# Difference products in the second attention: scores of a key tile added to those of the tile two before, still in the bank

## The reference, cut to what matters

```
q = (text_hidden @ Wq) -> (b, 16, 256, 128)
k = (vision_tokens @ Wk), v = (vision_tokens @ Wv) -> (b, 8, 1601, 128), each used by two heads
scores = q k^T / sqrt(128);  attn = softmax(scores);  out = (attn v) @ Wo
```

## Time and profile before

| | us |
|---|---|
| median of 3 runs | 1743.28 |
| runs | 1741.46 to 1745.71 |
| the profiled execution | 1741.94 |
| its span (first to last instruction) | 1740.6 |

### The profile page before, as it was taken

One profiled execution on the slowest core, in us unless ns is written; L12 is line 12 of the kernel. 1 busy time (PEld: TensorE's weight loads), 2 busy tenths in 40 slices (PEclk: granted clock), 3 DMA queues, 4 the chain that ended last, 5 costly groups with the idle time before them and its releaser, 6 DMA issues.

```text
span 1740.6 us, 26277 instructions
## 1 busy us (share of the span) xinstructions
PE 1568.9 (90%) x8998; PEld 750.3 (43%) x8998; DVE 1290.8 (74%) x2579; ACT 1067.6 (61%) x1766; POOL 746.3 (43%) x571
## 2 busy tenths in 40 slices
PE   5788988989968799789999999999989999999989
PEld 3243343333323343224444554544544555455455
DVE  5777667767777146578889869899688886788937
ACT  3467767767756545447766656656567665666734
POOL 0013014014020012046687747776476665566723
PEclk8799999999989799979999999999999999999989
DMA  3000000000020130100000000000000000000000
GB/s 130 1 1 1 20 1 2 21 1 2 2 79 2 55 124 19 28 20 1 20 20 30 1 1 25 1 8 23 1 1 1 2 1 1 1 1 1 1 0 25
DMA packets 15883, 29.36 MB, mean 17 GB/s; under 512 B 2594, under 2 KB 12934, under 8 KB 14726
## 3 DMA queue, kind: packets, MB, share of 16 engines
q1 hardware_dynamic: 15750, 27.68, 4.7%
HBM read 26.53 MB, written 1.15 MB: 16 GB/s over the span
## 4 chain that ended last, share of the span: by engine, by line
PE 43%; DVE 7%; issue 5%; ACT 3%; POOL 1%; DMA 0%; DVEq 0%; POOLq 0%; ACTq 0%
PE BK L488 42%; DVE arena L1601 4%; DVE arena L1624 2%; ACT arena L1703 1%; POOL arena L1740 1%; ACT arena L1707 1%; DVE arena L1593 0%; ACT L1703 0%; ACT L731 0%; PE BK L1524 0%; PE BK L747 0%; DVE arena L1610 0%; ACT arena L1693 0%; DVE arena L1607 0%; DVEq L424 0%
## 5 line engine op out<-in xcount | busy, mean ns | idle before, releaser
L488 PE MATMUL BK<-arena 128*128 128x512 bf16 (+9 forms) x8670 | 1525.1, 370 | 115.0 <-DVE arena L1601 24.3
L488 PEld LDWEIGHTS BK<-arena 128*128 128x128 bf16 (+5 forms) x8670 | 715.3, 113 | 894.4 <-issue 263.1
L1740 POOL TENSOR_TENSOR arena<-arena 128x512 f32<-128x512 f32 (+1 forms) x352 | 505.4, 1436 | 224.0 <-ACT arena L1703 206.1
L1624 DVE TENSOR_TENSOR arena<-arena 128x512 bf16<-128x512 f32 (+1 forms) x416 | 431.0, 1040 | 23.4 <-ACT arena L1707 22.1
L1703 ACT ACTIVATE arena<-BK,arena 128x512 f32<-128x512 f32 (+1 forms) x416 | 285.8, 687 | 253.4 <-PE BK L488 253.4
L994 DVE TENSOR_REDUCE arena<-BK 128x1 f32<-128x512 f32 x384 | 251.2, 685 | 46.0 <-PE BK L488 44.2
L1136 ACT ACTIVATE arena<-BK 128x512 f32<-128x512 f32 (+1 forms) x416 | 225.7, 595 | 91.0 <-PE BK L488 86.2
L1601 DVE CUSTOM_DVE_ANT_0 arena<-BK,arena 128x512 bf16<-128x512 f32 x384 | 262.5, 684 | 22.8 <-PE BK L488 5.9
L1707 ACT CAST arena<-arena 128x512 bf16<-128x512 f32 (+1 forms) x416 | 257.1, 618 | 13.3
L1168 POOL TENSOR_TENSOR arena<-arena 128x256 f32<-128x256 f32 (+6 forms) x45 | 30.2, 672 | 180.6 <-ACT arena L1084 178.3
L1190 POOL TENSOR_TENSOR arena<-arena 128x512 bf16<-128x512 f32 x24 | 28.5, 1192 | 177.2 <-DVE arena L973 177.2
(11 more groups left out here) (150 smaller groups left out, 812.2 us busy)
## 6 DMA issues: line engine op xcount, KB each, us to landing
arena<-in_ctxT SPq DMA_DIRECT2D x8, 800.5 KB, 6.0
arena<-in_ctxk SPq DMA_DIRECT2D x4, 768.0 KB
arena<-in_wqT SPq DMA_DIRECT2D x1, 2048.0 KB, 10.2
arena<-in_wo SPq DMA_DIRECT2D x1, 2048.0 KB, 14.7
arena<-in_x SPq DMA_DIRECT2D x4, 256.0 KB, 11.3
arena<-in_rsel SPq DMA_DIRECT2D x1, 1024.0 KB, 9.5
arena<-in_rw1T SPq DMA_DIRECT2D x1, 1024.0 KB, 5.1
arena<-in_rwgT SPq DMA_DIRECT2D x1, 1024.0 KB, 7.6
```

The source lines that it names most:

```text
L488: return T.matmul(out_, lhsT, rhs, start=start, stop=stop, skip_group_check=True)
L1624: V.tensor_tensor(Pl[k][0:m, :], P1[k][0:m, :], Ph[k][0:m, :], ALU.subtract).then_inc(p_low, 1)
L1740: G.tensor_tensor(acc[0:m, g % 2, :], acc[0:m, g % 2, :], P1[k][0:m, :], ALU.add).then_inc(summed1, 1)
```

## The change

In the second attention, key tiles 0 and 1 are made as before, with the row of maxima as the first of their four products. From tile 2 on, three products are added (`start=False`) to the bank that still holds the scores of tile kt - 2, with the difference of the two context tiles in place of the context: differences `dch` (high part) and `ctl` (low part, columns from 256 on). The product with the row of maxima is made for kt 0 and 1 alone. The bank is now `kt % 2`, so kt 12 of one group and kt 0 of the next are both in bank 0.

The differences are made in the stage of the experts. `cx` now has on DVE: the cast to `cth`, a wait for POOL's low part of the first 256 columns, the difference of 1345 columns in float32 in place (in `ctf`), and its cast to `dch`; on POOL: the low part of the first 256 columns, and after DVE's cast that of the 1345. The context pieces start at step 12 (`s >= E - 4`), since three of the `dch` lie where the weights of the folding are, so `cx` falls behind `up` of steps 16, 21, 26 and 31.

Two more edits: `o1a` makes one column a product in place of 128, and the ternary intermediates `qa` and `qb_` become bfloat16.

```diff
@@ stage1
-            next(cside, None)
+            if s >= E - 4:
+                next(cside, None)
@@ stage2
-                piece("s1", s, bank=ntile[0] % 2)
-                ntile[0] += 1
+                piece("s1", s, bank=kt % 2)
@@ buffers
+        dch = [sb(f"dch{b}", [128, S2 - 256], BF16, L1) for b in range(3)] + [sb("dch3", [128, S2 - 256], BF16, MN)]
-        qa = sb("qa", [128, 1024], F32, L1)
-        qb_ = sb("qb_", [128, 1024], F32, L1)
+        qa = sb("qa", [128, 1024], BF16, L1)
+        qb_ = sb("qb_", [128, 1024], BF16, L1)
@@ vector_moe, piece cx
                     V.tensor_copy(cth[:, b, :], ctf[b % 2]).then_inc(ct_high, 1)
+                    dve.wait_ge(ct_done, 2 * b + 1)
+                    V.tensor_tensor(ctf[b % 2][:, 0:S2 - 256], ctf[b % 2][:, 256:S2], ctf[b % 2][:, 0:S2 - 256],
+                                    ALU.subtract).then_inc(ct_step, 1)
+                    dve.wait_ge(ct_step, b + 1)
+                    dve.wait_ge(*emptied("fold", H - 1))
+                    V.tensor_copy(dch[b][:, :], ctf[b % 2][:, 0:S2 - 256]).then_inc(ct_step_high, 1)
@@ gpsimd_moe, piece cx
-                    G.tensor_tensor(ctl[:, b, :], ctf[b % 2], cth[:, b, :], ALU.subtract).then_inc(ct_done, 1)
+                    G.tensor_tensor(ctl[:, b, 0:256], ctf[b % 2][:, 0:256], cth[:, b, 0:256], ALU.subtract).then_inc(ct_done, 1)
+                    pool.wait_ge(ct_step_high, b + 1)
+                    G.tensor_tensor(ctl[:, b, 256:S2], ctf[b % 2][:, 0:S2 - 256], dch[b][:, :],
+                                    ALU.subtract).then_inc(ct_done, 1)
@@ sync_moe, piece cxl
-                    sp.wait_ge(ct_done, b - 1)
+                    sp.wait_ge(ct_done, 2 * b - 2)
@@ tensor_l1, piece s1
+                    high = cth[:, b, ks] if kt < 2 else dch[b][:, 128 * kt - 256:128 * kt - 256 + m]
                     pe.wait_ge(*emptied("qp", g))
-                    mm(o, cth[:, b, ks], qh[:, r, :], stop=False)
-                    mm(o, cth[:, b, ks], ql[:, r, :], start=False, stop=False)
-                    mm(o, ctl[:, b, ks], qh[:, r, :], start=False, stop=False)
-                    pe.wait_ge(rows1[g % 2], 16 * (g // 2 + 1))
-                    mm(o, onb[:, 0:m], mrw[:, g % 2, :], start=False).then_inc(full[i], 1)
+                    if kt < 2:
+                        pe.wait_ge(rows1[g % 2], 16 * (g // 2 + 1))
+                        mm(o, onb[:, 0:m], mrw[:, g % 2, :], stop=False)
+                    mm(o, high, qh[:, r, :], start=False, stop=False)
+                    mm(o, high, ql[:, r, :], start=False, stop=False)
+                    mm(o, ctl[:, b, ks], qh[:, r, :], start=False).then_inc(full[i], 1)
@@ tensor_l1, piece o1a
-                        t = mm(BK[6][:, 128 * u:128 * u + 128], acc[:, g % 2, 128 * u:128 * u + 128], ones[:, :])
+                        t = mm(BK[6][:, u:u + 1], acc[:, g % 2, 128 * u:128 * u + 128], ones[:, 0:1])
@@ vector_l1, piece o1a
-                    V.tensor_scalar(dn[:, 0:4], BK[6][:, :].rearrange("p (u n) -> p u n", u=4)[:, :, 0], 1e-30, None,
-                                    ALU.max).then_inc(free[6], 1)
+                    V.tensor_scalar(dn[:, 0:4], BK[6][:, 0:4], 1e-30, None, ALU.max).then_inc(free[6], 1)
```

More of the change, by code:

```diff
@@ L588, in program @@
         ckl = sb("ckl", [128, B, NKT, 128], BF16, CK)
+        junk = sb("junk", [128, 512], BF16, CK)
+        dch = [sb(f"dch{b}", [128, S2 - 256], BF16, L1) for b in range(3)] + [sb("dch3", [128, S2 - 256], BF16, MN)]
         mcb = sb("mcb", [128, B, NKT], F32, L1)
@@ L595, in program @@
         ones = sb("ones", [128, 128], F32, L1)
-        onb = sb("onb", [128, 128], BF16, L1)
+        onb = sb("onb", [128, 128], BF16, CT)
         mrw = sb("mrw", [128, 2, 512], BF16, L1)
@@ L600, in program @@
         ql = sb("ql", [128, 3, 512], BF16, L1)
-        junk = sb("junk", [128, 512], BF16, L1)
         mtl = sb("mtl", [128, 4, TAIL], F32, L1)
@@ L620, in program @@
         hs_ = sb("hs_", [128, 3, 2], F32, L1)
-        on1 = sb("on1", [128, 128], F32, L1)
+        on1 = sb("on1", [128, 128], F32, CT)
         F1 = Region(base, 107 * KB)
@@ L1246, in program @@
                              "dn_done", "ct_done", "ct_high"))
+        ct_step, ct_step_high = sem("ct_step"), sem("ct_step_high")
         ac_done = sem("ac_done")
```

## The result

| | before | after |
|---|---|---|
| median, us | 1743.73 | 1770.26 |
| runs, us | 1741.46 to 1745.71 | 1766.19 to 1772.52 |
| the profiled execution, us | 1741.94 | 1768.56 |

The changed kernel is slower by 1.5%: ratio 1.015, 95% interval 1.0125 to 1.0174. The forecast was 1706, within 1686 to 1728. The median before is now that of four runs.

The account below looks back on a forecast made before the run. PE was taken to set the pace up to about 93% DVE load, DVE at some 95%. 1741.9 - 47 (groups) + 3 (edges) + 0.65 (row) + 6.1 (experts) = 1704.7, median 1706, range 1686 to 1728, chance 0.86.

Parts of the forecast that it names:

- eight bare: Groups 19 to 21, 23, 26 to 29 of the second attention: 2.0 us gained each, 16.0 together.
- Removed on PE: Second attention: 11 of 13 tiles lose one 0.216 us product, 2.37 us a group, 75.9 if nothing else bound.
- What DVE and POOL then do: Bare group: 0.4 us more DVE work, pair's turn 1.6 us, 94% share; 23.95 us, so 2.0 gained.
- PE waiting for DVE's maxima: Sign that the forecast is right: PE waits for DVE's maxima or low parts in more groups; no size given.
- Slower: POOL keeps DVE from the shared path: Rival, second attention: each 0.1 us more per mean low part adds 1.3 us DVE a group; 1790 at 0.3; chance 0.04.
- POOL and DVE exclude each other fully: Rival, second attention: no overlap, 25.2 us a group with POOL's diagonal, median 1741, no change; chance 0.03.
- PE alone bounds: Rival, second attention: all 75.9 us of removed products are gained, median 1674; chance 0.05.
- Sum over the 32 groups: Second attention: gains added by kind of group, together 47 us, bounds 62 and 25.
- Group edge: kt 0 waits for bank 0 from the exp of kt 12: 0.1 us, or 3 us over 31 edges, bounds 0 and 12.
- o1a: Products of one column in place of 128 gain 0, as weight loads stay; bounds 0 and 0.9 us a group.
- Experts: DVE's cx block of 4.4 us delays steps 16, 21, 26, 31 by 1.9, 2.4, 1.5, 0.3: 6.1 us, bounds 2 and 11.
- Row first: Group 0: three products now follow the row's DMA instead of running while it came, 0.65 us lost once.

Follow-up runs that it names:

- e6: Kernel after with the transpose of the maxima one turn later, the turns of a group kept at 18: 1731.01 us, ratio 0.9922.
- e14: Kernel after with POOL's sums over 256 of 512 columns, the other half left out: 1685.77 us, ratio 0.9674.
- e2: Kernel after with POOL's sums over 16 of 512 columns, the rest left out: 1670.54 us, ratio 0.9579.
- e13: Kernel after with the third of three maxima of a query block reading 16 of 512 columns: 1723.88 us, ratio 0.9881.
- e7: Kernel after with POOL's sum of a tile waiting for DVE's low part of that tile: 1854.36 us, ratio 1.0627.
- e1: Kernel after with the bank alternating over all tiles again, also across the group edge: 1768.65 us, ratio 1.0145.
- e9: Kernel after with e6 (transpose one turn later), e8 (context block over three steps) and e1 (alternating banks) together: 1724.44 us, ratio 0.9895.
- e8: Kernel after with DVE's context block split over three steps (cast; difference; cast): 1764.60 us, ratio 1.0119.

## Why the prediction was wrong

The profiled executions differ by 26.6 us; forecast were -37.2. Of the 63.8 us between, some 58 are in the second attention, 5 ahead of its first exp, 1 behind its last. By the groups of the sum (change of their time in us, from the starts of the exps of kt 0; the forecast column is without the 3 us for the edges, the measured ones hold them):

| groups | forecast | after | e6 | e14 |
|---|---|---|---|---|
| eight bare | -16.0 | +2.5 | -13.7 | -19.6 |
| three with the projection | -6.6 | +2.5 | +1.0 | -2.8 |
| 7, 12, 18 | -4.5 | +0.8 | -4.1 | -6.5 |
| 11, 15 | -1.2 | -0.6 | -1.2 | -3.5 |
| 30, 31 | -1.6 | +1.7 | +1.8 | -5.5 |
| 0 | -0.7 | +0.2 | 0.0 | -2.2 |
| eight as 22 | -12.0 | +4.0 | -5.3 | -17.0 |
| five ternary | -4.5 | +2.5 | -2.0 | -8.8 |

- **Removed on PE: right.** 0.216 us a product and 23.6 us of PE work a group; e2 and e14 run at 23.48 when nothing else holds PE, 0.09 of it for `o1a`.
- **What DVE and POOL then do: the step that failed, twice.** First its size. I took 0.4 us more DVE work a group; it was 1.5 (23.4 in place of the 22.3 I reckoned with). I had 1.6 us for the pair's turn, from four sums in 6.47 us, a stretch that begins with an unslowed sum and leaves out the pause behind the last. Where both engines always have work waiting, POOL's sums in fact start 1.68 us apart (at 1648.66, 1650.34 and 1652.03 in the same group 31 before). That is more than the mean step of 1.58, so the pair was not "just able to follow", and it is still more over the dense steps behind kt 8, 10 and 11, which take 1.51; averaging over ten steps hid these. From kt 8 to the edge POOL runs sum on sum. Of the twelve low parts of 128 keys in group 20 after, four take 1.64 to 1.75 us, two 1.14 and six 0.67 to 0.76; one of the four stands just ahead of the tail that the transpose waits for, another ahead of the maxima at the edge. Second, the measure. I turned DVE's work into time by a share of 94%, read from groups 11 and 20. The share alone doesn't decide: PE waited with DVE at 89% (after and e13), and e6 runs with DVE at 94%. What decides is whether DVE has done a certain piece when PE, with its queue in order, arrives there. Before, PE had eight products more in the ten steps up to the transpose, 1.7 us; they were DVE's head start. The forecast had "PE waiting for DVE's maxima" among its signs, but priced no place of it.
- **Slower: POOL keeps DVE from the shared path (given 0.04): the mechanism that came,** with the low part lengthened by half of what it was priced for. The low part grew by 0.138 us; by my 95% that should have left a gain in bare groups, and they lost 0.3 us instead. POOL's sum didn't hold up each low part either: four in twelve were held for some 1.0 us and two for 0.46. The transpose, which e6 shows to be worth 2.04 us a bare group, was missing from it. The Trainium skill (SBUF — State Buffer, "Who interferes with whom") has the order of issue decide who is blocked. The trace agrees in direction: the same low part takes 0.68 us with POOL idle and 1.74 behind a sum that has just begun (1364.84 behind 1364.76), while e7 shows the reverse order to be worse here. It doesn't agree that the block lasts for the whole instruction: a turn of both takes 1.68 us, less than the two one behind the other.
- **POOL and DVE exclude each other fully (0.03): falls.** With the diagonal it asks for 25.2 us a group; e6 runs bare groups in 24.23, group 30 takes 22.4, and where both engines have work waiting a turn is 1.68 us, not 1.28 + 0.68.
- **PE alone bounds: falls,** but e14 shows what it would have been worth: with half of POOL's sums, bare groups reach it. No version here did so with the sums whole.
- **Sum over the 32 groups.** The three with the projection were "filled by PE" only at kt 9 to 11; they have the same transpose as the others, and rose by 2.5 us instead of falling by 6.6. Of the 2.5, 1.7 are the shared bank's and 0.85 the clock's, at the end of group 24; with alternating banks (e1) the three are at -0.1. Groups 30 and 31 were to gain 0.8 each; in group 31 the gap behind kt 7 grew from 3.03 to 7.04 us, with no maxima left to make. There the exps come 1.30 us apart and POOL's sums 1.68, so POOL comes late to its diagonal, and PE waits for it (3.4 us behind that wait ran at the lower clock, too; in e1, at full clock, the gap is 5.51):
```profile
1680.05 8.18 PE L488 MATMUL BK<-arena 128*128 128x512 f32 x26 [3.06 <-POOL arena L1758]
```
- **A term that was missing: the clock in the second attention.** Before, the granted clock is at full from 762 us to the end of this stage. In the kernel after it falls from full in seven short stretches, 30.6 us together, 10.2 of them in group 14, 6.8 in group 17 and the rest in groups 0, 24, 25 and 31; one of them is
```profile
1182.00:1189.00 7.00, 7.00 (x24) 5.17 (x22) 3.46 (x5) 1.30 (x2) 5.04 (x4) 0.52 0.43 135
```
Group 14 rose by 2.6 us, and in e6 and e9, where its clock stayed at full, it fell by 1.7; group 17 rose by 2.0, and in e2, likewise at full, it fell by 3.5 (with POOL's work gone too). So some us of the table's row of five ternary groups (the last), and of the differences between runs in it, are the clock's, and not the products'. The bare groups, on which the account rests, ran at 1.00 throughout. Why the clock fell there was not tried.
- **Group edge: wrong in its cause and in its size.** I took 0.1 us at each of 31 edges for a wait on bank 0. e1 shows none in bare groups and some 0.6 us at each of the three edges behind a projection. What the bare groups' edges did lose, 1.5 us each, is the maxima's.
- **o1a: right within its bounds** (0.09 us a group, where 0 was taken and 0.9 was the bound).
- **Experts: the block was right, its echo too small.** 4.1 us against 4.4 forecast; 7.9 us came of it by the last L1401 against 6.1, and e8's 5.7 us given back agree with the block as their cause. Another 3.9 us were lost between there and the first exp of the second attention. 2.5 of them are in float32 products of the first queries: eight took 2.81 us in place of 1.97, and ten more 4.11 in place of 2.43; 1.2 are the row's (next point). In the windows of the ten, after and then before, the granted clock differs:
```profile
742.00:746.00 4.00, 4.00 (x10) 2.77 (x10) 0.00 (x0) 0.28 (x1) 0.00 (x0) 0.57 0.20 57
```
```profile
733.00:735.50 2.50, 2.43 (x10) 1.63 (x10) 0.00 (x0) 0.42 (x1) 0.00 (x0) 1.00 0.68 195
```
The ten ran at near the lower of the clock's two levels (1.2 GHz) instead of at the higher (2.4 GHz). PE had stood idle for 1.55 us before both. Why the clock fell only in the one case was not tried.
- **Row first: too low.** In group 0 PE waits 2.88 us for the row's DMA, before 1.70 with three products already made, and the three come after it. From the transpose to the first exp it takes 5.16 us in place of 3.99, so 1.2 us and not 0.65. The 0.216 us a product were taken at full clock, and the granted clock of this stretch is 0.50.

What stays open: why the clock falls where it does, how the loss of the groups with more DVE work splits between it and the waits, and whether a kernel could have both engines' waits gone at once (e2 and e14 leave work out; e9, the best whole kernel, keeps 0.8 us a bare group and the ternary groups' load).

## What to carry to other kernels

When work is taken off an engine whose queue is in order, look up every point at which it will now arrive earlier, and price each by what the other engine does just before: a share of busy time doesn't tell it. The work that was removed may have been the head start of another engine; a late piece that feeds a loop (here the transpose, the queries, the maxima) costs more than its own wait, and moving that one piece by a turn returned 2.04 of the 2.8 us that a bare group had lost here. And for two engines that hinder each other, take the turn from a stretch in which both always have work waiting, and compare it with the shortest steps of the third engine, not with the mean: that the loss begins where the turn outgrows the step fits these runs, but no run measured the point.

## What was not expected of the hardware

- The low part on DVE takes 0.68 us alone and up to 1.75 beside POOL's sums run one behind the other, which themselves go from 1.27 to 1.53. A turn of both is 1.68 us, 0.14 of it a pause of POOL, and so 0.27 less than 1.27 and 0.68 in a row.
- POOL's shortest sums take 0.22 us for 16 columns (e2), 0.72 for 256 (e14) and 1.26 for 512 (after). By these three some 0.2 us of each, an estimate, doesn't depend on the columns.
- The maximum (L1614), which reads a PSUM bank and a mask in SBUF, kept 0.684 us as a mean before and after, and never took more than 0.70, however busy POOL was. The low part, with both inputs in SBUF, was slowed.
